# Two-layer cross-attention kernel: batches 2 to 4 take ranks and router logits by columns, and GpSimd makes low parts of x, u and the keys

## The reference

```
logits = x @ router_W.T + router_b            # 8 per token
w      = softmax(logits)
a_sum  = sum_j x @ ctx_4096[j].T              # 64 ranks per token, summed over the batch axis of ctx
y      = einsum('bsr,nhr->bsnh', a_sum, lora_B)
out    = x + 0.5 * sum_n w[n] * y[n]          # then NaN to 0 and infinities to +-1e4
```

## Time and profile before

| | |
|---|---|
| median of three runs | 639.76 us (639.5 to 642.15) |
| the profiled execution | 639.82 us, span 638.0 us, mean granted clock 0.996 |
| TensorE busy | 628.6 us, 99% of the span |
| VectorE busy | 498.2 us, 78% |
| ScalarE busy | 337.6 us, 53% |
| GpSimd busy | 268.0 us, 42%, 20 us of it in the first 300 us |
| DMA | 114.1 MB, mean 179 GB/s |

### The profile page before, as it was taken

How to read it: one execution, slowest core, us unless ns; L and a number is a source line. 1 busy time by engine, 2 the same in 40 slices (tenths; PEclk the granted TensorE clock), 3 DMA queues, 4 the chain that set the end, 5 groups by cost and what they waited for, 6 DMA issues and landing times.

```text
span 638.0 us, 10730 instructions
## 1 busy us (share of the span) xinstructions
PE 628.6 (99%) x3455; PEld 544.4 (85%) x3455; DVE 498.2 (78%) x907; ACT 337.6 (53%) x999; POOL 268.0 (42%) x358
## 2 busy tenths in 40 slices
PE   9999999999999999999999999999999999999995
PEld 8988889888988889888788888888888888888884
DVE  5789995578457773677568899999999999999834
ACT  5453453123242232323258777777778777777621
POOL 0120001000030002000325556788899888888956
PEclk9999999999999999999999999999999999999998
DMA  8945595436874467721857993534355354523132
GB/s 316 408 127 173 176 300 190 155 83 205 241 253 160 115 221 246 279 98 38 269 129 282 373 389 107 149 94 148 115 127 179 97 175 111 150 99 117 59 107 100
DMA packets 103399, 114.14 MB, mean 179 GB/s; under 512 B 57008, under 2 KB 76080, under 8 KB 103344
## 3 DMA queue, kind: packets, MB, share of 16 engines
q1 hardware_dynamic: 103008, 113.07, 53.9%
q10 hardware_dynamic: 336, 0.39, 0.2%
HBM read 67.29 MB, written 46.14 MB: 178 GB/s over the span
## 4 chain that ended last, share of the span: by engine, by line
PE 96%; DVE 2%; issue 1%; DMA 0%; ACT 0%; POOL 0%; DVEq 0%; POOLq 0%; ACTq 0%
PE ps L602 26%; PE ps L603 26%; PE ps L604 26%; PE ps L664 4%; PE ps L747 4%; PE ps L760 2%; PE ps L761 2%; PE ps L636 1%; PE ps L638 1%; PE ps L635 1%; PE ps L674 1%; DMA stage<-WkT 0%; DVE u_lo L891 0%; DVE cx_sum L987 0%; PE ps L627 0%
## 5 line engine op out<-in xcount | busy, mean ns | idle before, releaser
L1268 POOL TENSOR_TENSOR u_sb<-a_sb,w_sb 128x512 f32<-128x512 f32 x16 | 19.6, 1246 | 235.3 <-DVE w_sb L885 230.4
L602 PE MATMUL ps<-wo_hi,cx_hi 128*128 128x512 f32 (+1 forms) x264 | 105.9, 401 | 0.0
L1194 ACT ACTIVATE s_sb<-s_sb,s_min 128x64 f32<-128x64 f32 x256 | 85.8, 339 | 34.6 <-DVE s_min L965 34.6
L604 PE MATMUL ps<-wo_hi,cx_lo 128*128 128x512 f32 (+1 forms) x264 | 101.7, 385 | 0.0
L603 PE MATMUL ps<-wo_lo,cx_hi 128*128 128x512 f32 (+1 forms) x264 | 101.6, 385 | 0.0
L602 PE MATMUL ps<-act_hi,w_hi 128*128 128x512 f32 x256 | 100.9, 394 | 0.3 <-DVE q_sb L939 0.3
L603 PE MATMUL ps<-act_lo,w_hi 128*128 128x512 f32 x256 | 99.9, 390 | 0.0
L604 PE MATMUL ps<-act_hi,w_lo 128*128 128x512 f32 x256 | 99.8, 390 | 0.0
L1159 ACT ACTIVATE act_hi<-h_t 128x512 fp32r<-128x512 f32 x32 | 20.3, 633 | 111.6 <-DVE h_t L928 111.6
L987 DVE SCALAR_TENSOR_TENSOR cx_sum<-ps,bias_c,cx_raw 64x256 f32<-64x256 f32 x128 | 61.8, 483 | 8.8 <-ACT cx_raw L1208 4.8
L1279 POOL TENSOR_TENSOR s_sb<-s_sb,s_inv 128x512 f32<-128x512 f32 x64 | 67.1, 1048 | 0.0
(11 more groups left out here) (120 smaller groups left out, 1538.9 us busy)
## 6 DMA issues: line engine op xcount, KB each, us to landing
q_cols<-q_sb SPq DMA_DIRECT2D x32, 512.0 KB, 3.6
qb<-q_cols SPq DMA_DIRECT2D x64, 256.0 KB, 3.9
x_sb<-xT SPq DMA_DIRECT2D x32, 256.0 KB, 3.0
h_rows<-hn_sb SPq DMA_DIRECT2D x64, 128.0 KB, 3.0
output_weights<-wo_sb SPq DMA_DIRECT2D x32, 256.0 KB, 2.7
z_sb<-h_rows SPq DMA_DIRECT2D x16, 512.0 KB, 4.5
out<-z_sb SPq DMA_DIRECT2D x15, 512.0 KB, 2.9
stage<-WvT SPq DMA_DIRECT2D x8, 512.0 KB, 4.7
```

What stands on the lines that cost most here:

```text
L602: pe.matmul(dst, lh, rh, start=(first and j == 0), stop=False)
L604: mm = pe.matmul(dst, ll, rh, start=False, stop=(last and j == n - 1))
L1194: act.activation(s_sb[c % 4][:, h, :], s_sb[c % 4][:, h, :], ACT.Exp, bias=s_min[c % 2][:, h:h + 1], scale=-1.0, accum_out=s_sum[c % 2][:, ...
```

## The change

For batches 2 to 4 (i = 1 to 3) the ranks and the logits are computed with features on the contracted side and tokens on the columns. ScalarE makes a high part of each of the 8 chunks of x (`x_parts`), GpSimd the low part, in three buffers that lie in the memory of u; `tokens` is three matmuls of 512 columns for each chunk, into one bank. The stationary tile holds 64 ranks, 56 columns of low parts and the 8 logits, so the result's lower half is added to its upper half. `spread` copies the bank out, transposes the 32 rows with the logits on VectorE, does the softmax there on 32 partitions, splits the weights in high and low part and turns them back; `weigh` is ScalarE's copy of the turned weights. `grow` replaces `expand`: four matmuls with four contracted rows each spread the weights over the 128 rows of a chunk of u, VectorE multiplies them by the ranks (u_f), ScalarE makes the high part of u and GpSimd the low part. GpSimd also makes the low parts of the keys, for all four batches, and builds constants at the start. Batch 1 keeps the old way.

The places in the list move as well: `leave` of the first half stands ahead of `grow`; every batch's updates start two queries into the second half, as only batch 2's did before, and end with two updates in a row; key parts 2 and 3 stand after `spread` and after `weigh`; of the eight half chunks of output weights in a batch, which all stood beside the first half of its queries or right behind it, three are left there and five stand in the second half, in batches 1 and 2, the first five of all now in batch 1; the mask is loaded at the start of batch 1's queries. k_hi has two buffers instead of four. In the diff the constants, the adapter's parts and most of the softmax are left out.

```diff
-    out += [("values_out",)] + up(0, 7, split("Q", 5, 4))
-    beside = {0: {1: [("last_low", 0)] + split("Q", 6, 7) + [("flush", 0, 6), ("key_parts", 0)], 2: [("flush", 0, 7), ("key_parts", 1)],
-                  3: split("Q", 2) + [("mask",), ("key_parts", 2)], 4: split("Q", 3) + [("key_parts", 3)], 5: [("route", 1)]}}
+    out += [("values_out",)] + up(0, 7, split("Q", 5, 4) + parts(1, 0, 1, 2))
+    beside = {0: {0: [("mask_in",)],
+                  1: [("last_low", 0)] + split("Q", 6, 7) + [("flush", 0, 6), ("key_parts", 0)],
+                  2: [("flush", 0, 7), ("key_parts", 1)] + tokens(1, 0, 1, 2) + parts(1, 3, 4, 5),
+                  3: split("Q", 2) + tokens(1, 3, 4) + parts(1, 6, 7) + [("mask",)],
+                  4: split("Q", 3) + tokens(1, 5, 6, 7) + [("spread", 1)], 5: [("key_parts", 2)],
+                  6: [("weigh", 1), ("key_parts", 3)]}}
     for i in range(1, NB):
         beside[i] = {n: [("last_low", i)] * (n == 1) + [("flush", i, 5 + n)] * (n in (1, 2)) for n in range(KC)}
         if i < NB - 1:
-            beside[i][3] += [("route", i + 1)]
-            beside[i][5] += [("expand", i + 1, 0)]
-            beside[i][6] += [("expand", i + 1, 1)]
-            for n in range(KC - 1):
-                beside[i][n] += [("output_weight", KC * (i - 1) + n)]
+            beside[i][1] += tokens(i + 1, 0, 1, 2) + parts(i + 1, 3, 4, 5)
+            beside[i][2] += [("output_weight", 8 * i - 3)]
+            beside[i][3] += tokens(i + 1, 3, 4) + parts(i + 1, 6, 7) + [("output_weight", 8 * i - 2)]
+            beside[i][4] += tokens(i + 1, 5, 6, 7) + [("output_weight", 8 * i - 1)] + [("spread", i + 1)]
+            beside[i][6] += [("weigh", i + 1)]
     for i in range(NB):
         for n, k in enumerate(Q_FIRST if i == 0 else range(KC)):
             out += [("query", i, 0, k)] + beside[i].get(n, [])
             if i == NB - 1 and n == 1:
                 return out
         out += leave(i, 0, 0) + leave(i, 0, 1)
-        if 0 < i < NB - 1:
-            out += [("output_weight", KC * i - 1)]
-        late = 1 if i == 0 else 0
-        if i == 0:
-            out += [("expand", 1, 0)]
+        out += [("grow", i + 1)]
         for k in range(KC - 1):
             out += [("query", i, 1, k)]
             if k == 0 and i == 0:
-                out += [("expand", 1, 1), ("output_weight_in",)]
-            if k >= late:
-                out += up(i + 1, k - late)
+                out += [("output_weight_in",)]
+            if k:
+                out += up(i + 1, k - 1)
+            if i < NB - 2 and k >= 2:
+                out += [("output_weight", 8 * i + k - 2)]
         held = out.pop()
         out += [("query", i, 1, KC - 1)] + leave(i, 1, 0) + [held]
-        if late:
-            out += up(i + 1, KC - 2, leave(i, 1, 1))
-        else:
-            out += leave(i, 1, 1)
-        out += up(i + 1, KC - 1)
+        out += up(i + 1, KC - 2, leave(i, 1, 1))
+        out += up(i + 1, KC - 1, parts(i + 2, 0, 1, 2) if i + 2 < NB else ())
...
+        x_hi = [at(f"x_hi{k}", [P, TOK], AT_U + 4096 * k, F32R) for k in range(3)]
+        x_lo = [at(f"x_lo{k}", [P, TOK], AT_U + 4096 * k + 2048, F32R) for k in range(3)]
+        w_rows = at("w_rows", [P, TOK], AT_U + 12288, F32R)
+        u_f = [at(f"u_f{k}", [P, TOK], AT_U_SB + 2048 * k) for k in range(2)]
+        k_hi = [at(f"k_hi{k}", [P, KC, V], AT_WO_SB + 2048 * (k % 2), F32R) for k in range(NB)]
+        ps_w = [ps[:, k, :] for k in (4, 6, 7, 5)]
...
+            def tokens(i, k):
+                x_h, x_l, n = x_hi[k % 3][:], x_lo[k % 3][:], KC * (i - 1) + k
+                if k == 0:
+                    wait(pe, u_made, RC * (i - 1))
+                pe.wait_ge(xlo_done, n + 1)
+                pe.matmul(ps_a, a_w[0][:, k, :], x_h, start=(k == 0), stop=False)
+                pe.matmul(ps_a, a_w[0][:, k, :], x_l, start=False, stop=False)
+                pe.matmul(ps_a, a_w[1][:, k, :], x_h, start=False, stop=(k == KC - 1)).then_inc(a_mm, 1)
+            def grow(i):
+                pe.wait_ge(route_act, 3 * i + 1)
+                pe.wait_ge(t_ready, KC * i)
+                for j in range(RC):
+                    rows = slice(B * j, B * j + 4)
+                    pe.matmul(ps_w[j], choose[rows, :], w_rows[rows, :], start=True, stop=True).then_inc(w_mm, 1)
...
-                if c == 0:
-                    pe.wait_ge(ulo_done, TT * (i + 1))
+                if m == 0:
+                    pe.wait_ge(ulo_done, TT)
                 wait(pe, t_ready, m - 1)
                 cols = slice(c * P, (c + 1) * P)
-                three(ps_up[c % 2], [(b_hi[:, j, cols], b_lo[:, j, cols], u_hi[:, j, :], u_lo[:, j, :])
-                                     for j in range(RC)]).then_inc(up_mm, 1)
+                for j in range(RC):
+                    if c == 0 and i:
+                        pe.wait_ge(ulow_done, RC * (i - 1) + j + 1)
+                    mm = three(ps_up[c % 2], [(b_hi[:, j, cols], b_lo[:, j, cols], u_hi[:, j, :], u_lo[:, j, :])],
+                               first=(j == 0), last=(j == RC - 1))
+                mm.then_inc(up_mm, 1)
...
-            def key_parts(b):
-                dve.wait_ge(khi_done, b + 1)
-                dve.tensor_tensor(k_lo[:, b, :, :], k_full[:, b, :, :], k_hi[b][:], ALU.subtract).then_inc(klo_done, 1)
...
+            def spread_weights(i):
+                done = ROUTE_0 + ROUTE * (i - 1)
+                bc = [QUAD.stop - QUAD.start, BLOCKS, NR]
+                dve.wait_ge(route_act, 3 * i - 1)
+                dve.transpose(lg_blocks[QUAD], a_t[QUAD].rearrange("p (t n) -> p t n", n=B)).then_inc(route, 1)
...
+                dve.tensor_tensor(a_t[0:LOW, :], a_t[0:LOW, :], a_t[R:R + LOW, :], ALU.add).then_inc(route, 1)
+                dve.wait_ge(route_act, 3 * i)
+                dve.tensor_reduce(lg_sum[QUAD], lg[QUAD], AX_X, ALU.add).then_inc(route, 1)
...
+                weights = lg[QUAD].rearrange("p t (j s) -> p t j s", s=2)
+                dve.tensor_copy(w_split[QUAD, :, :, 0:2], weights).then_inc(route, 1)
...
+                for j in range(RC):
+                    dve.tensor_copy(w_blocks[B * j:B * j + B, :, 0:4], w_split[QUAD, :, j, :]).then_inc(route, 1)
+                dve.wait_ge(route, done + 14)
+                dve.transpose(w_turned[:].rearrange("p (t n) -> p t n", n=B), w_blocks[:]).then_inc(route, 1)
+                dve.tensor_copy(a_t[R:P, :], a_t[0:R, :]).then_inc(route, 1)
+            def grow(i):
+                dve.wait_ge(route, ROUTE_0 + ROUTE * i)
+                for j in range(RC):
+                    dve.wait_ge(w_mm, RC * (i - 1) + j + 1)
+                    if j >= 2:
+                        dve.wait_ge(ulow_done, RC * (i - 1) + j - 1)
+                    dve.tensor_tensor(u_f[j % 2][:], ps_w[j], a_t[:], ALU.mult).then_inc(u_made, 1)
...
-                if b == NB - 1:
-                    act.wait_ge(mask_step, 4)
+                if b >= 2:
+                    act.wait_ge(k_stored, 32 * b)
...
+            def x_parts(i, k):
+                act.wait_ge(x_in[k // 2], 32 * (i + 1))
+                act.wait_ge(up_mm, KC * i)
+                if k >= 3:
+                    act.wait_ge(a_mm, KC * (i - 1) + k - 2)
+                act.activation(x_hi[k % 3][:], x_sb[:, k, :], ACT.Copy).then_inc(xhi_done, 1)
+            def spread_exp_of(i):
+                act.wait_ge(a_mm, KC * i)
+                act.activation(a_t[:], ps_a, ACT.Copy).then_inc(route_act, 1)
+                act.wait_ge(route, ROUTE_0 + ROUTE * (i - 1) + 4)
+                act.activation(lg[QUAD], lg[QUAD], ACT.Exp).then_inc(route_act, 1)
+            def weigh(i):
+                act.wait_ge(route, ROUTE_0 + ROUTE * i - 1)
+                act.activation(w_rows[:], w_turned[:], ACT.Copy).then_inc(route_act, 1)
+            def grow(i):
+                for j in range(RC):
+                    act.wait_ge(u_made, RC * (i - 1) + j + 1)
+                    act.activation(u_hi[:, j, :], u_f[j % 2][:], ACT.Copy).then_inc(uhi_done, 1)
...
+            def x_parts(i, k):
+                if k == 0:
+                    if i == 1:
+                        pool.wait_ge(ulo_done, TT)
+                    wait(pool, ulow_done, RC * (i - 1))
+                    pool.memset(w_blocks[:], 0.0).then_inc(w_clear, 1)
+                pool.wait_ge(xhi_done, KC * (i - 1) + k + 1)
+                pool.tensor_tensor(x_lo[k % 3][:], x_sb[:, k, :], x_hi[k % 3][:], ALU.subtract).then_inc(xlo_done, 1)
+            def key_parts(b):
+                pool.wait_ge(khi_done, b + 1)
+                pool.tensor_tensor(k_lo[:, b, :, :], k_full[:, b, :, :], k_hi[b][:], ALU.subtract).then_inc(klo_done, 1)
+            def grow(i):
+                for j in range(RC):
+                    if j == 2:
+                        pool.wait_ge(w_mm, RC * i)
+                    if j == 3:
+                        pool.wait_ge(u_made, RC * i)
+                    pool.wait_ge(uhi_done, RC * i + j + 1)
```

(49 more changed lines are left out.)

129 lines of the change are left out of this document (81 added, 48 removed).

## The result

| | before | after |
|---|---|---|
| median of the runs, us | 639.83 (4 runs, 639.5 to 642.15) | 659.73 (4 runs, 659.65 to 659.87) |
| profiled execution: time, span | 639.8, 638.0 | 659.73, 657.6 |
| TensorE's clock, mean of the span | 0.996 | 0.985 |

The changed kernel is slower: ratio 1.0298, 95% interval 1.0281 to 1.0315. 649.1 was predicted, with 655 as the upper end. The sign was right; the forecast loss was 9.3 us, the measured one 19.9 us.

What follows compares the result with a forecast made beforehand. TensorE's instruction stream, without holes, was taken as the bound. Losses of 6.6 + 5.2 + 1.2 + 3.0 + 0.9 = 16.9 us against 7.6 gained gave +9.3 on 639.8, so 649.1 us; range 636 to 655.

Steps and rivals of the forecast that it cites:

- gained on TensorE: Batches 2 to 4: old passes and transposes go, 8.89 us a batch, new matmuls cost 6.35; 7.6 us gained in all.
- stalls 1 and 2: TensorE waits in batch 1's first queries, for Q5's low part, then for x_lo 3 and 4; 6.6 us, 5.6 to 7.8.
- stall 3: Second half of batch 1's queries: first query copy waits on ScalarE for all key stores, holding up TensorE 5.2 us.
- lower clock: TensorE's clock falls after the idle stretch before the second half of batch 1's queries; 1.2 us, 0 to 2.
- stall 4: End of batches 2 and 3: x_lo 0 to 2 of the next batch come late, 1.5 us twice, 3.0 in all.
- rows of u, scores: Low parts of u late by 0.15 us a batch, second phase's start 0.4 later; together 0.9 us, 0 to 2.
- stall 5: Not forecast: TensorE's waits for query copies at the end of the updates of batches 2 and 3, 3.06 us each.
- Rival (d): VectorE, held up by turns, becomes the bound of the updates; 653 us at 0.3 more for 14 chunks; chance 0.02.
- stall 2: Batch 1's first queries: x_lo 3 stands behind keys 0 and 1 on GpSimd, x_lo 4 follows; 4.6 us, 3.2 to 4.8.
- stall 1: Batch 1's first queries: Q5's low part on VectorE is late through turns with GpSimd's x_lo; 2.0 us, between 0.95 and 3.1.
- GpSimd's 1.30 us: Price taken for each 512-column low part GpSimd makes, from a row with two full inputs at 1299 ns.
- rows 6: Old profile's rows of VectorE subtractions beside GpSimd products, read as the two engines taking turns by whole instructions from 30.04 on.

Runs made afterwards that it cites:

- e1: Changed kernel with each output weight between its update and its select instead of behind the select; 654.42 us.
- e4: Changed kernel, same order, with the output weights' low part made by GpSimd instead of VectorE; 654.54 us.
- e5: Changed kernel with output weights between update and select, and key parts 2 and 3 made early; 649.08 us.
- e3: Changed kernel with key parts 2 and 3 right behind the last split of Wq, key 2's high part in its own memory; 653.69 us.
- e6_x_parts_later: Changed kernel with the first three x_hi and x_lo of batch 2 moved behind the last select of batch 1's updates; 660.59 us.
- c1: Changed kernel with weights between, key parts 2 and 3 early, 0 and 1 on VectorE, first x parts, batch 2's logits and batches 3 and 4's first tokens later; 648.78 us.

## Why the prediction was wrong

Terms of the sum, read from the trace after (81 to 340 us):

| | predicted | measured |
|---|---|---|
| gained on TensorE | 7.6 | 8.3 |
| stalls 1 and 2 | 6.6 | 6.4 (2.4, 2.55, 1.4) |
| stall 3 | 5.2 | 5.2 |
| lower clock | 1.2 | 4.2 |
| stall 4 | 3.0 | 2.0 |
| rows of u, scores | 0.9 | 1.4 + 0.3 |
| stall 5 | 0 | 6.1 |

- **The step that failed** is "In the update loops VectorE had 0.90 us idle per 5.44; an output weight takes 0.61. Cover is left, at no cost". I compared a duration with an idle time, and did not ask what the weight's low part waits for on its engine. It waits 1.22 us for ScalarE. e1 and e4 each take that wait away in another manner, and stall 5 goes both times. The 6.1 are two times 3.06; this term alone takes 649.1 to 655.2, and the 3.0 us of clock beyond the 1.2 forecast to 658.2. Rival (d) named VectorE as the bound of the updates and gave it 0.02, since "GpSimd is idle there". It was idle, for 44.1 us up to 176.38, and VectorE became the bound without it.
- **The clock** was mis-sized: 21 matmuls at 0.427 in place of 0.227, 4.2 us. I had it fall in stall 3 alone; it fell after stall 2 as well, and after the first stall 5 (not the second), 1.4 us each time. Where it falls differs between executions: stall 1 is 2.4 us in all of them, and the clock fell behind it in e1 to e4, but not in the changed kernel and e5.
- **Stalls 1 and 2** came out as costed in the sum, 6.4 for 6.6, by some luck: stall 1 was 0.4 over its 2.0, and stall 2 0.6 under its 4.6. Finite 0.71 and bound 1.51 show that one-input operations take turns too. With them the prediction's walk had Q5 ready at 89.65, and TensorE went on at 89.43; it had asked at 87.03, 0.46 later than in the old trace, which is most of what lies between 3.1 and 2.4. By the rule of the Trainium skill ("SBUF — State Buffer", section Who interferes with whom) the two-port mode takes the lock also for a one-source tensor_scalar; the trace agrees (bound takes 0.42 alone and 1.51 beside x_lo).
- **Stall 3** was right in its links. From ScalarE's copy at 109.23 to the query at 122.96 it is 13.7 us (14.3 predicted), and TensorE wanted the bank after 8.5 (9.1 predicted). ScalarE waited for the landing of the key stores (e3 takes it away):

```profile
121.44 2.42 ACT L1295 ACTIVATE q_sb<-ps,bias_c 128x512 fp32r<-128x512 f32 x4 [3.99 <-DMA keys<-k_lo]
```

- **Stall 4** was 0.31 in batch 3 and 1.7 in batch 4, where 1.5 was predicted for each. Stall 5 stood ahead of both; only the slow stretch behind the first one differs. Without stall 5, in e1, both are 1.7, and in e6_x_parts_later, where the clock fell at the second stall 5 and not at the first, batch 3 has 1.7 and batch 4 0.6. So it was the lower clock that hid it, by bringing TensorE to x_lo later.
- **Rows of u** were costed at 0.15 a batch. TensorE waited for the low parts of the third and fourth chunk, 0.3 and 0.45 us, in batches 3 and 4. The scores' 0.3 is near the 0.4 of the sum.
- **The gain.** Ranks and logits are 5.45 a batch, and the four small matmuls run from 117.28 to at most 0.44 later, where batch 3 resumes (201.21 to 201.65): 5.9 a batch, where 6.35 were predicted; the old passes and transposes were 8.64, 8.89 with what follows them. Four pitches would be 0.9, and one is 0.227. By the rule cited from the Trainium skill ("TensorEngine Tiling (Array Packing)", section Tiling Modes, Key Properties) they run in parallel; the trace agrees in that 0.44 is less than half of the four pitches, though it is not the one pitch that the prediction made of the rule.
- **GpSimd's 1.30 us** was right alone (u_lo 1.29); beside VectorE x_lo took 1.45 in the mean. The turns that the prediction reads from rows 6 end at 33.3 and 34.4 us by its own durations, the rows at 33.07 and 34.15: they fit to 0.3 us, not exactly. The rows:

```profile
L1429 POOL TENSOR_TENSOR x_lo<-x_sb,x_hi 128x512 fp32r<-128x512 f32 x24 | 34.1, 1452 | 139.2 <-ACT x_hi L1250 139.2
...
L1443 POOL TENSOR_TENSOR u_lo<-u_f,u_hi 128x512 fp32r<-128x512 f32 x12 | 15.3, 1291 | 34.1 <-ACT u_hi L1265 34.1
```

The table's net is 17.3 us of the 19.6 between the spans. 0.4 is lost ahead of 81 us, and the first matmul after a wait or a change of shape stands 0.1 us longer before the next, 21 times against 11 before (1.1 us more). The rest, under 1 us, I did not separate.

## What to carry to other kernels

Before an operation is put into idle time of an in-order engine, find what it waits for there: its wait, not its duration, is what the queue behind it pays, and the payment may show much later, where a buffer's slack runs out (here some 27 us). Check an engine's period in a loop against TensorE's, not its busy share. Here TensorE had no holes, and a change that took work off it and lengthened the chains around it gave the gain back. A stall that is taken away can come back one place later, as in c1, so measure the sum.

## What was not expected of the hardware

- Four matmuls of 4 contracted rows on row groups 0, 32, 64 and 96 took 0.44 us together, with 512 columns each; one of 128 rows takes 0.227.
- In the changed kernel the clock fell inside stall 3 (granted 1.00 at 118 to 119 us, 0.50 at 120 to 121), and 0.7 and 1.2 us after matmuls had resumed behind stall 2 (2.4 and 1.25 us without them) and the first stall 5 (2.9); it came back after about seven matmuls at 0.427. After the second stall 5, of the same length, it did not fall, nor after stall 1 (2.25), behind which it fell in e1 to e4. What decides no run here settles.
- GpSimd and VectorE slow each other also where VectorE's operation has one input from SBUF: bound's 0.42 became 1.51. Eight x_lo, of the same shape as u_lo's 1.29, took 15.3 us beside a VectorE that was busy for 13.9 of them.
